# A graph-attention and mixture-of-experts kernel: the first expert tile computed inside the routing block

## What is computed

```python
x = x + gnn(layernorm(x))                    # two attention layers over the edges
xf = layernorm(x)
ggates, gidx = top2(xf @ Wg + bg)            # 2 of 4 groups, softmax over the chosen
egates, eidx = top4(xf @ We[g] + be[g])      # 4 of 8 experts in each group
combine = gw[:, :, None] * ew                # 8 experts per row, gates under 1e-6 are zero
for g, e: h = gelu(xf @ W1[g, e] + b1[g, e]) # 768 -> 384
          y += combine[:, g, e] * (h @ W2[g, e] + b2[g, e])   # 384 -> 768
x = x + y
```

## Time and profile before

| what | value |
|---|---|
| median of the runs | 1523.4 us |
| span of the profiled execution, first to last instruction | 1518.7 us |
| own time of the profiled execution | not given beside its span |
| TensorE busy (matmul) | 1360.8 us, 90% |
| VectorE busy | 1160.0 us, 76% |
| ScalarE busy | 737.2 us, 49% |
| GpSimd busy | 505.1 us, 33% |
| mean granted TensorE clock | 0.971 of 2.4 GHz |
| first lists | 796 us |
| routing block's barrier | 810 us |
| last scatter issued | 1507 us |

### The profile page before, as it was taken

How to read it: one execution, slowest core, us unless ns; L and a number is a source line. 1 busy time by engine, 2 the same in 40 slices (tenths; PEclk the granted TensorE clock), 3 DMA queues, 4 the chain that set the end, 5 groups by cost and what they waited for, 6 DMA issues and landing times. The chain is left out here.

```text
span 1518.7 us, 31335 instructions
## 1 busy us (share of the span) xinstructions
PE 1360.8 (90%) x7728; PEld 1135.4 (75%) x7739; DVE 1160.0 (76%) x1823; ACT 737.2 (49%) x1171; POOL 505.1 (33%) x557
## 2 busy tenths in 40 slices
PE   6888888888778889889977999999999999999995
PEld 4555656733223348889967999999999999999995
DVE  6499999899999988858878477555565655888882
ACT  3556465255555553422224455444454544666662
POOL 1000000003333410032324555555465555555563
PEclk9999999799999999999977999999999999999998
DMA  6300001041222214233566987867778876799963
GB/s 233 138 18 9 18 28 61 18 179 61 73 95 63 78 44 141 63 105 106 127 166 216 269 223 204 186 166 170 171 193 205 203 191 159 210 271 273 254 135 49
DMA packets 102255, 211.68 MB, mean 139 GB/s; under 512 B 19318, under 2 KB 58486, under 8 KB 102082
## 3 DMA queue, kind: packets, MB, share of 16 engines
q1 hardware_dynamic: 79186, 142.06, 28.7%
q0 software_dynamic: 22240, 66.69, 22.0%
q10 hardware_dynamic: 784, 2.36, 0.4%
HBM read 164.14 MB, written 54.93 MB: 144 GB/s over the span
## 5 line engine op out<-in xcount | busy, mean ns | idle before, releaser
L992 PE MATMUL ps_o<-prob,h_head 128*97 128x512 f32 (+1 forms) x480 | 187.7, 528 | 51.5 <-DVE prob L934 51.5
L2070 POOL DMA_INDIRECT out_nodes<-y,to_index x92 | 160.1, 1740 | 133.9 <-issue 73.5
L2387 PE MATMUL ps_h<-e_hi,e_xt_hi 128*128 (+1 forms) x546 | 192.6, 353 | 6.3 <-ACT e_xt_hi L2189 3.6
L992 PEld LDWEIGHTS ps_o<-prob,h_head 128*97 128x97 f32 x480 | 73.2, 164 | 165.4 <-issue 89.7
L2372 PE MATMUL ps_y<-e_hi,e_ht_hi 128*128 (+1 forms) x546 | 191.6, 351 | 3.6 <-DVE e_ht_lo L2305 2.2
L2387 PE MATMUL ps_h<-e_lo,e_xt_hi 128*128 (+1 forms) x546 | 184.7, 338 | 0.0
L2372 PE MATMUL ps_y<-e_hi,e_ht_lo 128*128 (+1 forms) x546 | 183.6, 336 | 0.0
L2372 PE MATMUL ps_y<-e_lo,e_ht_hi 128*128 (+1 forms) x546 | 183.5, 336 | 0.0
L2254 DVE TENSOR_TENSOR e_lo<-raw,e_hi (+1 forms) x189 | 175.6, 950 | 7.3 <-ACT e_hi L2197 6.7
L2207 ACT ACTIVATE y<-ps_y,gate 128x768 f32 (+1 forms) x91 | 82.2, 903 | 192.4 <-PE ps_y L2372 124.2
L826 ACT ACTIVATE score<-score,al_col 128x1250 f32<-128x1250 f32 x80 | 106.0, 1335 | 98.4 <-DVE score L877 98.4
...
## 6 DMA issues: line engine op xcount, KB each, us to landing
...
```

The costliest lines, as they stand in the source:

```text
L992: turn = nc.tensor.matmul(ps_o[u][0:C1 + 1, c, 0:WID[c]], h_head[:, u, t, :], prob[:, t % 2, 512 * c:512 * c + WID[c]], start=(t == 0), st ...
L2070: nc.gpsimd.indirect_dma_start(out, bass.IndirectOffsetOnAxis(to_index[:, w:w + 1], 0), y[:, w, :], None, bounds_check=NP - 1, oob_is_err= ...
L2387: nc.tensor.matmul(ps_h[:, 0:HID], xt_hi[:, c, :], b[:, bass.ds(e % 2, 1), c * HID:(c + 1) * HID] .rearrange("p o m -> p (o m)"), start=(c ...
```

## The change

Inside the routing block now: the copy of tile 0's rows, its transposes, split, first product, the transposes of tile 1, the gather of tile 2, the rounded part of expert 0's second weights, and the load of the Gelu table (a dummy Gelu of one column). The first gathers read the list in place. Expert 1's loads and bias 0 are issued behind the store of tile 9's x2, ahead of the last stores into the table; expert 2's loads wait for the third gather. The order of the lists, of the splits and of the copies changes on VectorE and TensorE in both blocks; list 3 is matched in `first_tile` and summed and kept with tile 1. Most renamings are left out of the diff.

```diff
+                    if t == NT - 1:
+                        load_bias(sp, s, b1, 0)
+                        for piece in range(3):
+                            sp.wait_ge(s.w1_in[piece], 16)
+                            load_first(sp, s, w1, 1, piece)
+                        for piece in range(3):
+                            sp.wait_ge(s.w2_in[piece], 16)
+                            load_second(sp, s, w2, 1, piece)
...
-                for piece in range(3):
-                    sp.wait_ge(s.w1_in[piece], 16)
-                    load_first(sp, s, w1, 1, piece)
-                for piece in range(3):
-                    sp.wait_ge(s.w2_in[piece], 16)
-                    load_second(sp, s, w2, 1, piece)
+                sp.wait_ge(s.b1_in, 16)
+                load_bias(sp, s, b1, 1)
...
-                pool.wait_ge(list_kept, 1)
-                nc.gpsimd.tensor_copy(s.index[:, :], s.list_i[:, LEAD:LEAD + 1]).then_inc(index_set, 1)
                 for u in range(2):
                     pool.wait_ge(xf_out[u], 16 * (NT // 2))
                 pool.wait_ge(gates_out, 16 * NT)
                 pool.wait_ge(filled, 5)
-                pool.wait_ge(index_set, 1)
+                pool.wait_ge(list_kept, 1)
                 nc.gpsimd.indirect_dma_start(s.landing[:, 0, :], None, s.table.ap(),
-                                             bass.IndirectOffsetOnAxis(s.index[:, 0:1], 0),
+                                             bass.IndirectOffsetOnAxis(s.list_i[:, LEAD:LEAD + 1], 0),
                                              bounds_check=NP - 1, oob_is_err=False).then_inc(s.gathered, 16)
...
                 pool.wait_ge(list_kept, 2)
-                nc.gpsimd.tensor_copy(s.index_1[:, :], s.list_i[:, LEAD + 1:LEAD + 2]).then_inc(index_set, 1)
-                pool.wait_ge(index_set, 2)
                 nc.gpsimd.indirect_dma_start(s.landing[:, 1, :], None, s.table.ap(),
-                                             bass.IndirectOffsetOnAxis(s.index_1[:, 0:1], 0),
+                                             bass.IndirectOffsetOnAxis(s.list_i[:, LEAD + 1:LEAD + 2], 0),
                                              bounds_check=NP - 1, oob_is_err=False).then_inc(s.gathered_1, 16)
+                pool.wait_ge(s.gathered, 16)
+                nc.gpsimd.tensor_copy(s.gate_0[:, :], s.landing[:, 0, D:TW]).then_inc(consts, 1)
+                pool.wait_ge(list_kept, 3)
+                pool.wait_ge(s.rows_kept, 1)
+                pool.wait_ge(consts, 20)
+                nc.gpsimd.indirect_dma_start(s.landing[:, 0, :], None, s.table.ap(),
+                                             bass.IndirectOffsetOnAxis(s.list_i[:, LEAD + 2:LEAD + 3], 0),
+                                             bounds_check=NP - 1, oob_is_err=False).then_inc(s.gathered, 16)
...
                 exp(NT - 1)
-                for t in range(NT - 2, NT):
-                    split_gates(t)
-                    keep_bias(t)
+                for piece in range(3):
+                    act.wait_ge(s.w2_in[piece], 16)
+                    at = piece * PIECE
+                    nc.scalar.activation(s.e2_hi[:, 0, at:at + PIECE], s.raw2[:, 0, at:at + PIECE], ACT.Copy)
+                split_gates(NT - 2)
+                keep_bias(NT - 2)
+                split_gates(NT - 1)
+                nc.scalar.activation(gelu_row[:, :], half_neg[:, :], ACT.Gelu)
+                act.wait_ge(s.x_turned, 1)
+                nc.scalar.activation(s.xt_hi[:, :, :].rearrange("p (b k) n -> p b (k n)", b=2),
+                                     s.ps_first[:, :, 0:HALF], ACT.Copy).then_inc(s.x_hi_made, 1)
+                keep_bias(NT - 1)
...
+                def keep_rows(k, landed):
+                    dve.wait_ge(landed, 16)
+                    nc.vector.tensor_copy(s.in_rows[:, :], s.landing[:, k, 0:D]).then_inc(s.rows_kept, 1)
...
+                start = dve.value_load(s.starts[0:1, 1:2], min_val=LEAD, max_val=LIST - NT)
+                keep(1, start)
                 rest_of_gates(NT - 2)
                 rest_of_weights(0)
-                start = dve.value_load(s.starts[0:1, 1:2], min_val=LEAD, max_val=LIST - NT)
-                keep(1, start)
+                keep_rows(0, s.gathered)
+                rest_of_weights(1)
+                rest_of_weights(2)
+                dve.wait_ge(s.x_hi_made, 1)
+                nc.vector.tensor_tensor(s.xt_lo[:, :, :].rearrange("p (b k) n -> p b (k n)", b=2),
+                                        s.ps_first[:, :, 0:HALF],
+                                        s.xt_hi[:, :, :].bitcast(F32).rearrange("p (b k) n -> p b (k n)", b=2),
+                                        ALU.subtract).then_inc(s.x_lo_made, 1)
+                rest_of_gates(NT - 1)
+                keep_rows(1, s.gathered_1)
                 match(2)
-                rest_of_gates(NT - 1)
-                rest_of_weights(1)
+                dve.wait_ge(tiles_summed, 2)
+                nc.vector.tensor_tensor(s.before_row[:, :], ps_sums[0:1, P:P + LIST], any_row[:, :], ALU.add)
                 start = dve.value_load(s.starts[0:1, 2:3], min_val=LEAD, max_val=LIST - NT)
                 keep(2, start)
-                rest_of_weights(2)
-                dve.wait_ge(tiles_summed, 2)
-                nc.vector.tensor_tensor(s.before_row[:, :], ps_sums[0:1, P:P + LIST], any_row[:, :], ALU.add)
...
+                def turn_x(k):
+                    pe.wait_ge(s.rows_kept, k + 1)
+                    if k:
+                        pe.wait_ge(s.x_lo_made, k)
+                    for c in range(KD):
+                        last = nc.tensor.transpose(s.ps_first[:, c // 3, (c % 3) * P:(c % 3 + 1) * P],
+                                                   s.in_rows[:, c * P:(c + 1) * P], s.ident[:, :])
+                    last.then_inc(s.x_turned, 1)
+
+                def first_product():
+
+                    pe.wait_ge(s.x_hi_made, 1)
+                    for b in (s.e1_hi, s.e1_lo):
+                        for c in range(KD):
+                            if b is s.e1_lo and c % 2 == 0:
+                                pe.wait_ge(w1_lo_ready, c // 2 + 1)
+                            nc.tensor.matmul(s.ps_h[:, 0:HID], s.xt_hi[:, c, :], b[:, 0, c * HID:(c + 1) * HID],
+                                             start=(c == 0 and b is s.e1_hi), stop=False)
+                    pe.wait_ge(s.x_lo_made, 1)
+                    for c in range(KD):
+                        last = nc.tensor.matmul(s.ps_h[:, 0:HID], s.xt_lo[:, c, :],
+                                                s.e1_hi[:, 0, c * HID:(c + 1) * HID],
+                                                start=False, stop=(c == KD - 1))
+                    last.then_inc(s.h_summed, 1)
...
                 turn_gates(NT - 1)
-                turn_nothing(nc, s, ps_l[:, 0:P], 8)
+                turn_x(0)
+                turn_nothing(nc, s, s.ps_h[:, 0:P], 3)
+                first_product()
+                turn_x(1)
+                list_now(2)
                 weigh_bias(NT - 1)
-                list_now(2)
-                turn_nothing(nc, s, ps_l[:, 0:P], 18)
...
+                if start:
+                    with eng.If(tiles > 1):
+                        one(e, 1, early=True)
+                    with eng.If(tiles < 2):
+                        first_alone()
...
-                load_bias(sp, s, b1, 0)
-                sp.wait_ge(b1_in, 16)
-                load_bias(sp, s, b1, 1)
+                sp.wait_ge(gathered, 32)
...
-                pool.wait_ge(gathered, 16)
-                keep_gates(0, 0).then_inc(gate_kept, 1)
-                next_index(LEAD + 2).then_inc(index_set, 1)
-                pool.sem_inc(index_set, 1)
-                pool.wait_ge(rows_kept, 1)
-                pool.wait_ge(index_set, 2)
-                gather(0)
+                nc.gpsimd.tensor_copy(gate[:, 0, :], gate_0[:, :]).then_inc(gate_kept, 1)
+                pool.sem_inc(index_set, 2)
...
-                pool.wait_ge(third_kept, 2)
+                pool.wait_ge(early_kept, 2)
...
+                def first_tile():
+
+                    split_x(1)
+                    act.wait_ge(biased, 1)
+                    nc.scalar.activation(h_act[:, :], h_in[:, :], ACT.Gelu).then_inc(gelued, 1)
+                    act.wait_ge(h_turned, 1)
+                    nc.scalar.activation(ht_hi[:, :, :].rearrange("p k n -> p (k n)"), ps_t[:, 0:HID],
+                                         ACT.Copy).then_inc(h_hi_made, 1)
+                    weights(1, 0)
+                    weights(1, 1)
...
+                def first_tile():
+
+                    dve.wait_ge(b1_in, 16)
+                    add_bias(0, 0)
+                    split_x(1)
+                    rest_of_h(0)
+                    match(AHEAD - 2, 1, early_made)
+                    weights(0, 1, (0,))
+
+                def second_tile(k, e):
+
+                    add_bias(k, e)
+                    keep_early()
+                    keep_rows(2)
```

(49 more changed lines are left out.)

146 lines of the change are left out of this document (91 added, 55 removed).

## The result

The changed kernel takes 1538.24 us (1537.92 to 1538.53, 4 runs) against 1523.67 us of the kernel before on the same chip (1522.79 to 1525.23, 4 runs): ratio 1.0088, 95% interval 1.0075 to 1.0100. By the medians that is 14.6 us slower; their quotient is 1.0096, and the ratio as recorded is somewhat smaller (13.4 us). 1534.1 was forecast, with a range of 1526.0 to 1539.0; the result lies inside it, near its upper end, and 0.7 us above the forecast's own narrower range of 1530 to 1537.5. The profiled execution's own time is 1538.24 us, its span 1536.5.

The account below looks back on a forecast made before the run. TensorE bounds the kernel from the second expert on, so a late start counts: tile 3 12.6 us late, less 1.95 idle, gives +10.7 on 1523.4: 1534.1 us. Range for 8 in 10: 1526.0 to 1539.0; own range 1530 to 1537.5.

Parts of the forecast that it names:

- rival 4: Moved loads, unfinished before 793, hold back the table's last stores; first gather up to 4 us later: +14.7, 1538.1; chance 0.10.
- Loads free: Expert 1's moved loads end about 789 to 791, ahead of the last gates at 793, and cost nothing.
- First product from 806.6 to 811.4: Tile 0's product in the routing block, 18 matmuls, starts behind ScalarE's x_hi and takes 4.8 us; bounds -1.6 to +1.6.
- Table load: ScalarE loads the Gelu table in 1.28 us, dummy done at 805.75; the skill's extra 1.38 us drain is left out.
- List 2 and third gather at 813.2 and 814.1: Routing block: list 2 is kept at 813.2, behind tile 0's product; GpSimd's third gather waits for it, +0.94 us.
- Drain of 4.8, exit at 819.5: GpSimd's drain after the third gather takes 4.8 us, barrier and first VectorE instruction 0.6; routing block's exit 8.8 us later.
- Rival 1: GpSimd's drain costs nothing when the gather is short: exit about 816.0, later steps 3.5 us earlier, +7.2, 1530.6; chance 0.15.
- Gates of tile 2 behind list 3 and 3.8 us of registers: Behind the barrier, list 3 kept at 828.2, then GpSimd's uncovered 3.8 us of registers; gates kept at 832.3.
- rival 2: Faster: registers ahead of GpSimd's wait, warm product, exit at 816.0; tile 2 at 827.4, 3.2 us early: 1520.2; chance 0.09.
- Gather of tile 3: 4.4 us, as the loads of expert 3 are held by late splits: Behind the barrier, tile 3's gather starts at 834.3, takes 4.4 us, lands at 838.7; bound 0 to +2.7.
- Given back 1.95: TensorE's 1.95 us of idle between 842 and 862 us absorbs that much of tile 3's 12.6 us lateness.
- Rivals 3 and 4: Rival 3: the late start is repaid by TensorE's 8.1 us of later idle; +2.6, 1526; chance 0.08.

Follow-up runs that it names:

- b_loads_only: Kernel before with only SP's six loads of expert 1 moved ahead of the last stores into the table: ratio 0.9991 to before.
- a_best: Changed kernel with lists 2 and 3 earlier, registers before the wait, splits before tile 3's rows, aligned row buffers, expert 2's loads in the routing block: 1.0018 of before.
- a_hold_loads3: Changed kernel with SP's loads of expert 3 begun only when the gather of tile 3's rows has landed: ratio 1.0080 to before.

## Why the prediction held, point by point

The forecast case came about, by the path that it named: late list 2, third gather, drain, late list 3, registers, gather of tile 3, splits. It cost 14.6 us in place of 10.7. That is inside the range, which took in rival 4 (1538.1, almost the measured time); rival 4's path, a first gather up to 4 us late, is not what happened, so that this number fits is chance. Times of after are set against the forecast's, each taken 1.0 us earlier for the earlier list 0.

- **Loads free**: right for the time (b_loads_only), wrong in the reason. They should have ended before the last gates were stored; the DMA share is still 1.03 from 793 to 794 us, and the store landed with list 0. So the first gather came at 797.08, 0.5 us later than foretold, as GpSimd had waited for that store. Nothing else came late by it, as tile 0's product waited for ScalarE, behind the table.
- **First product from 806.6 to 811.4**: start right (805.58), length 5.9 in place of 4.8 us, as it ran at the granted clock of 0.50 (1.2 GHz). That is +1.1, within the bound of +1.6.
- **Table load**: the dummy Gelu starts at 804.63, 0.02 behind the table's end at 804.61. ScalarE was busy until the load began. The extra drain that the Trainium skill has, in ScalarE: Activation LUTs, What ACT_TABLE_LOAD costs, isn't seen on either side of it.
- **List 2 and third gather at 813.2 and 814.1**: 813.1 and 813.88, with the shift of 1.0 us each 0.8 to 0.9 late, from the longer product.
- **Drain of 4.8, exit at 819.5**: 4.55, and 818.83; the size is right. The reason given, a price for leaving a block whatever is in flight, isn't shown: the drain ends just behind the gather's data, and a price of 4.5 us counted from the drain's start would end at the same time, within 0.1 us. Where the gather lands later, in a_best, the drain ends later with it (last section). So the size was right partly by luck: the queues were as empty as in before. Rival 1 had such a wait for the gather, but priced it at 0.3 us; its exit 3.5 us earlier didn't come.
- **Tile 1's product at 822.4**: 821.16, right. **Gates of tile 2 behind list 3 and 3.8 us of registers**: right as a row (list 3 at 827.58, copy at 831.47). Running the registers ahead, one of rival 2's conditions, gives 0.7 us alone.
- **Gather of tile 3: 4.4 us, as the loads of expert 3 are held by late splits**: this step is the term that was most mis-sized. SP issued those loads from 824.93 to 834.30, they weren't held, and the gather took 7.9 us (834.19 to 842.05, forecast 837.7). The earlier trace rows had shown 7.1 and stood as the upper bound; about the median was taken instead. Tile 2's product came 5.0 us later than foretold: 3.5 from this length, 0.9 from the later issue, 0.6 from VectorE between the copy of the gates and the last split. At tile 6 the lag is 15.2 us where the forecast has 10.7. That the gather's length is the whole of this difference isn't shown: a_hold_loads3 takes 2.4 us off it and wins 1.6 at tile 6.
- **Given back 1.95**: from tile 3 to tile 6 the lag shrank by 2.6 us, from 17.8 to 15.2.
- **In-place indices**: the three gathers' instructions took 1.10, 1.38 and 1.03 us against 1.12 and 1.54 in the earlier trace rows: the strided column costs them nothing.
- **Rivals 3 and 4**: the lag isn't repaid; from tile 6 to the last tile after takes 632.9 us and before 629.1. Rival 4's mechanism was there, with a late store and a first gather 0.5 us late, but not its 4 us. Both are out as accounts of the time.
